# Attention and ternary feed-forward on one core: steps without maxima as one group with a whole product, flags folded to one count, the last split of maxima ahead of VectorE's SBUF work

## The reference

```python
q, k, v = proj(wq, bq), proj(wk, bk), proj(wv, bv)      # (2, 16, 1024, 8) each
attn = softmax(einsum('bhqd,bhkd->bhqk', q, k) / sqrt(16))
a = einsum('bhqk,bhkd->bhqd', attn, v) -> (2, 1024, 128) @ wo.T + bo
x = layernorm(x + a)
h = silu((x @ w1.T) * w1_s) * ((x @ w2.T) * w2_s)        # hidden 512
h = gelu((h @ h1.T) * h1_s);  h = gelu((h @ h2.T) * h2_s)
x = layernorm(x + (h @ w3.T) * w3_s)
```

## Time and profile before

| what | value |
|---|---|
| median of 3 executions | 463.82 us (463.69 to 465.52) |
| the profiled execution, its own time | 464.68 us |
| its span | 462.9 us |
| TensorE busy | 449.7 us, 97% |
| VectorE busy | 399.0 us, 86% |
| ScalarE busy | 361.5 us, 78% |
| GpSimd busy | 87.6 us, 19% |
| granted TensorE clock, mean | 0.992 |

### The profile page before, as it was taken

One profiled execution on the slowest core, in us unless ns is written; L12 is line 12 of the kernel. 1 busy time (PEld: TensorE's weight loads), 2 busy tenths in 40 slices (PEclk: granted clock), 3 DMA queues, 4 the chain that ended last, 5 costly groups with the idle time before them and its releaser, 6 DMA issues.

```text
span 462.9 us, 9462 instructions
## 1 busy us (share of the span) xinstructions
PE 449.7 (97%) x3632; PEld 213.1 (46%) x3632; DVE 399.0 (86%) x450; ACT 361.5 (78%) x670; POOL 87.6 (19%) x138
## 2 busy tenths in 40 slices
PE   8999999999999999999999999999989999999994
PEld 5433333343333333333333333334343478877883
DVE  6899999999999999999999999999944377666736
ACT  3402898989988898998989889999968886677662
POOL 8400000000000000000000001254331081127103
PEclk9999999999999999999999999999989999999998
DMA  6667430500323060051304006031012000000101
GB/s 163 159 189 214 132 117 4 93 4 0 60 37 117 4 92 4 1 75 22 115 12 83 4 1 93 7 44 24 37 22 59 15 14 2 1 1 0 47 1 45
DMA packets 15547, 24.48 MB, mean 53 GB/s; under 512 B 4560, under 2 KB 8400, under 8 KB 15120
## 3 DMA queue, kind: packets, MB, share of 16 engines
q1 hardware_dynamic: 14864, 23.22, 21.8%
q10 hardware_dynamic: 640, 0.66, 0.7%
HBM read 14.82 MB, written 7.47 MB: 48 GB/s over the span
## 4 chain that ended last, share of the span: by engine, by line
PE 81%; DVE 10%; ACT 4%; DMA 1%; issue 1%; POOL 1%; ACTq 0%; POOLq 0%; DVEq 0%
PE ps L1049 32%; PE ps L1103 29%; PE ps L1190 15%; DVE negmax L805 8%; PE ps L1086 2%; ACT arena L547 2%; PE ps L1139 1%; DMA qx<-parts_q 1%; PE ps L1005 1%; ACT v_pad L583 1%; PE ps L1014 1%; PE ps L1073 1%; DMA parts_q<-arena 1%; PE ps L1157 1%; DVE hf L892 0%
## 5 line engine op out<-in xcount | busy, mean ns | idle before, releaser
L805 DVE TENSOR_REDUCE negmax<-ps 128x1 f32<-128x1024 f32 x256 | 309.5, 1223 | 5.6 <-PE ps L1049 2.7
L547 ACT ACTIVATE arena<-ps 128x512 f32<-128x512 f32 x512 | 275.1, 597 | 38.9 <-PE ps L1086 14.4
L1049 PE MATMUL ps<-kx,qx 61*128 61x512 f32 x512 | 186.3, 443 | 1.3 <-DVE negmax L805 0.9
L1086 PE MATMUL ps<-qx,kx 64*128 64x512 f32 x512 | 182.4, 450 | 0.0
L1103 PE MATMUL ps<-arena,v_pad 128*32 128x256 f32 x2048 | 163.7, 392 | 1.1 <-ACT arena L547 1.1
L1049 PEld LDWEIGHTS ps<-kx,qx 61*128 61x128 f32 x512 | 75.3, 184 | 100.4 <-DVE negmax L805 86.4
L1103 PEld LDWEIGHTS ps<-arena,v_pad 128*32 128x32 f32 x2048 | 40.3, 108 | 88.2 <-issue 51.4
L1086 PEld LDWEIGHTS ps<-qx,kx 64*128 64x128 f32 x512 | 75.8, 184 | 8.3 <-issue 5.1
L1190 PE MATMUL ps<-hid,w_high 128*128 128x512 f32 (+1 forms) x296 | 68.2, 387 | 0.8 <-issue 0.4
L1190 PEld LDWEIGHTS ps<-hid,w_high 128*128 128x128 f32 x296 | 54.2, 188 | 12.3 <-issue 0.8
L910 DVE TENSOR_TENSOR hid<-hf,hid 128x512 fp32r<-128x512 f32 x32 | 23.0, 727 | 20.2 <-ACT hid L599 20.2
(11 more groups left out here) (72 smaller groups left out, 228.4 us busy)
## 6 DMA issues: line engine op xcount, KB each, us to landing
kx<-parts_k SPq DMA_DIRECT2D x32, 128.0 KB, 3.7
qx<-parts_q SPq DMA_DIRECT2D x60, 64.0 KB, 3.8
late_sb<-in_late SPq DMA_DIRECT2D x3, 1280.0 KB, 5.7
parts_q<-prt SPq DMA_DIRECT2D x3, 512.0 KB, 4.5
parts_q<-arena SPq DMA_DIRECT2D x3, 512.0 KB, 5.1
xT_sb<-in_xT SPq DMA_DIRECT2D x4, 256.0 KB, 3.5
xT_sb<-arena SPq DMA_DIRECT2D x28, 32.0 KB
prt<-den SPq DMA_DIRECT2D x7, 128.0 KB
```

The costliest lines, as they stand in the source:

```text
L547: nc.scalar.activation(probs[:, n // HG % 2, heads(n), :], ps[:, PLAN["score", n][0], :], ACT.Exp, scale=SCALE).then_inc(exp_done, 1)
L805: nc.vector.tensor_reduce(negmax[:, t // TURNS % 2, h * QT + q:h * QT + q + 1], ps[:, bank:bank + 2, :], AX.XY, ALU.max, negate=True)\
L1049: ins = nc.tensor.matmul(ps[:, MAX_BANK + 2 * (t % 2) + part, :], qx[at, slot, qc, h, q * P:(q + 1) * P], kx[at, slot, h, part * C:(part + ...
L1086: nc.tensor.matmul(ps[:, bank, :], kx[at, slot, h % PAIR, kt * P:(kt + 1) * P], qx[at, slot, qc, h % PAIR, :], start=True, stop=True)\
```

## The change

**Groups.** From half 232 on (`TAIL_HALF`) a group is a whole step: four scores, then the product of the step before with all 512 queries in each of its matmuls. Before that nothing changes. The last turn of maxima moves from half 234 to the first such group, behind its scores.

**Banks.** Two banks that the turns used (4 and 5, `LATE_BANKS`) join the scores' rotation in place of one, and the scores go through five banks in turn. The x1 transposes and the count move to banks 2 and 3.

**Flags.** VectorE flags eight slices, adds them pairwise into one (bf16), flags the other three and adds them too (`fold`). TensorE does one count matmul over the folded slice in place of eleven. The count goes behind step 125 of the 128, the x1 transposes behind steps 121 and 122 (before: 123 and 125).

**VectorE's order.** `norm(0)` waits for the last split of maxima. Both chunks' statistics come first, then both normalisations, then the flags and folds around `split_x1`, then the reduction and `invert(2)`; `norm(2)` goes behind the gate tiles of chunk 1. ScalarE's copies of a unit or of the maxima go between the second and third exponential of a group.

```diff
-FIRST_BANKS, LATE_BANK = [7, 0, 6, 1], 5
+FIRST_BANKS, LATE_BANKS = [7, 0, 6, 1], (4, 5)
...
+TAIL_HALF = 2 * (TAIL - 1)
+GROUPS_ALL = TAIL_HALF + STEPS_ALL - (TAIL - 1)
+TURN_AT = {min(2 * KT * (w - 1) + THALF, TAIL_HALF): w for w in range(1, U_ALL)}
...
+def scores_of(h):
+    if h < TAIL_HALF:
+        return range(2 * h + HG, 2 * h + HG + 2)
+    return range((step_of(h) + 1) * HG, min((step_of(h) + 2) * HG, SCORES))
...
-                order.insert(0, LATE_BANK)
-                last[LATE_BANK] = ("reduced", U_ALL * TURNS)
+                order[:0] = LATE_BANKS
+                last.update({bank: ("reduced", U_ALL * TURNS) for bank in LATE_BANKS})
...
-WO_BANK, X1T_BANK, INEXACT_BANK = [2, 3, 6, 7], [2, 4, 6, 7], 4
+WO_BANK, X1T_BANK, INEXACT_BANK = [2, 3, 6, 7], [2, 3, 6, 7], 2
...
+            def fold(n, done):
+
+                nc.vector.tensor_tensor(nonzero[:, 0:n, :], nonzero[:, 0:n, :], nonzero[:, n:2 * n, :],
+                                        ALU.add).then_inc(flagged, 1)
+                dve.wait_ge(flagged, done)
...
+            dve.wait_ge(max_split, U_ALL)
             norm(0)
             norm(1)
-            flag(0, FLAGGED)
             first_stats(0)
+            first_stats(1)
             invert(1)
             first_apply(0)
+            first_apply(1)
+            flag(0, FLAGGED, 0, 1)
+            fold(4, 2)
+            split_x1(0)
+            split_x1(1)
+            fold(2, 3)
+            fold(1, 4)
+            flag(FLAGGED, SLICES, 1, 5)
+            fold(2, 6)
+            fold(1, 7)
             dve.wait_ge(counted, 1)
-            flag(FLAGGED, SLICES)
-            first_stats(1)
-            dve.wait_ge(counted, 2)
...
-            first_apply(1)
-            split_x1(0)
             invert(2)
-            split_x1(1)
-            norm(2)
...
+            norm(2)
...
-                at = slice(part * HALF, (part + 1) * HALF)
+                at = slice(0 if first else HALF, C if last else HALF)
...
-                for n in range(n0, n1):
-                    ins = nc.tensor.matmul(ps[0:1, INEXACT_BANK, :], ones[:], nonzero[:, n - n0, :],
-                                           start=(n == 0), stop=(n == SLICES - 1))
-                ins.then_inc(counted, 1)
+                pe.wait_ge(flagged, FOLDS)
+                pe.wait_ge(x1_split, 1)
+                nc.tensor.matmul(ps[0:1, INEXACT_BANK, :], ones[:], nonzero[:, 0, :],
+                                 start=True, stop=True).then_inc(counted, 1)
...
             BEHIND = {STEPS - 11: (out_proj, 0), STEPS - 10: (out_proj, 1),
-                      STEPS - 9: (count, 0, FLAGGED), STEPS - 6: (count, FLAGGED, SLICES),
-                      STEPS - 5: (turn_x1, 0), STEPS - 3: (turn_x1, 1)}
+                      STEPS - 7: (turn_x1, 0), STEPS - 6: (turn_x1, 1), STEPS - 3: (count,)}
```

More of the change, by code:

```diff
@@ L78, with step_of, unit_from @@
 HALF = C // 2
-HALVES_ALL = 2 * U_ALL * KT
+STEPS_ALL = U_ALL * KT
 SCORES = U_ALL * KT * HG
 TAIL = (U_ALL * TURNS - TURNS - LEAD + 1) // 2 + 1
-TURN_AT = {2 * KT * (w - 1) + THALF: w for w in range(1, U_ALL)}
+TAIL_HALF = 2 * (TAIL - 1)
+GROUPS_ALL = TAIL_HALF + STEPS_ALL - (TAIL - 1)
+TURN_AT = {min(2 * KT * (w - 1) + THALF, TAIL_HALF): w for w in range(1, U_ALL)}
 def heads(n):
     return ((1, 0, 3, 2), (1, 3, 0, 2))[n // HG >= TAIL][n % HG]
+def step_of(h):
+    return h // 2 if h < TAIL_HALF else h - TAIL_HALF + TAIL - 1
+def scores_of(h):
+    if h < TAIL_HALF:
+        return range(2 * h + HG, 2 * h + HG + 2)
+    return range((step_of(h) + 1) * HG, min((step_of(h) + 2) * HG, SCORES))
+def unit_from(h):
+    return step_of(h) // KT if step_of(h) % KT == 0 and (h >= TAIL_HALF or h % 2 == 0) and h >= 0 else None
 def bank_plan():
@@ L100, in bank_plan @@
     place(("max", 0))
-    for h in range(-2, HALVES_ALL - 2):
-        if h in TURN_AT:
+    for h in range(-2, GROUPS_ALL):
+        if h in TURN_AT and h < TAIL_HALF:
             place(("max", TURN_AT[h]))
-        for n in (2 * h + HG, 2 * h + HG + 1):
+        for n in scores_of(h):
             if n == TAIL * HG:
-                order.insert(0, LATE_BANK)
-                last[LATE_BANK] = ("reduced", U_ALL * TURNS)
+                order[:0] = LATE_BANKS
+                last.update({bank: ("reduced", U_ALL * TURNS) for bank in LATE_BANKS})
             place(("score", n))
[L109 to L118, removed]
+        if h in TURN_AT and h >= TAIL_HALF:
+            place(("max", TURN_AT[h]))
+        w = unit_from(h)
+        if w == 0:
+            plan["pv", w] = held, None
+        elif w is not None:
+            place(("pv", w))
+            order.remove(plan["pv", w][0])
+            order.insert(0, held)
+            last[held] = ("unit", w - 1)
+            held = plan["pv", w][0]
     return plan
 PLAN = bank_plan()
-WO_BANK, X1T_BANK, INEXACT_BANK = [2, 3, 6, 7], [2, 4, 6, 7], 4
+WO_BANK, X1T_BANK, INEXACT_BANK = [2, 3, 6, 7], [2, 3, 6, 7], 2
 GATE_BANKS, GELU_BANK = [(0, 2, 6), (0, 2, 4)], 4
@@ L131 @@
 PIECE = LATE // (ITERS - 1)
-FLAGGED = 8
+FLAGGED, FOLDS = 8, 7
 W_STEPS = range(0, 2 * SLICES, 2)
@@ L555, in copy_max, with copy_unit @@
                 nc.scalar.activation(mT[:, w % 2, :], turned(w), ACT.Copy).then_inc(max_copied, 1)
+            def copy_unit(w):
+                act.wait_ge(pv_done, (w + 1) * KT)
+                nc.scalar.activation(attn_flat[:, w * C:(w + 1) * C], ps[:, PLAN["pv", w][0], :], ACT.Copy)\
+                   .then_inc(unit_out, 1)
             copy_max(0)
-            for h in range(-2, HALVES_ALL):
-                if h in TURN_AT:
+            for h in range(-2, GROUPS_ALL):
+                if h in TURN_AT and h < TAIL_HALF:
                     copy_max(TURN_AT[h])
[L561 to L565, removed]
+                if h < TAIL_HALF and unit_from(h):
+                    copy_unit(unit_from(h) - 1)
+                for n in scores_of(h):
+                    exp(n)
+                    if h >= TAIL_HALF and unit_from(h) and n % HG == 1:
+                        copy_unit(unit_from(h) - 1)
+                    if h >= TAIL_HALF and h in TURN_AT and n % HG == 1:
+                        copy_max(TURN_AT[h])
+                k = step_of(h) - STEPS * (ITERS - 1)
+                if k in W_STEPS and (h >= TAIL_HALF or h % 2 == 1):
+                    n = W_STEPS.index(k)
                     if n == 0:
@@ L568, in _ @@
                     nc.scalar.activation(half(w_high[:, n, :]), w_sb[:, n, :], ACT.Copy).then_inc(w_rounded, 1)
[L569 to L574, removed]
+            warm(ACT.Silu)
+            copy_unit(U_ALL - 1)
             def silu(c, m):
```

41 lines of the change are left out of this document (21 added, 20 removed).

## The result

The changed kernel takes 458.04 us (median of 4 executions, 457.59 to 458.6), the kernel before in the same comparison 464.35 us (463.69 to 465.52). The ratio is 0.9856 with an interval of 0.9835 to 0.9877, so it is faster by 1.2 to 1.7%. Now and then an execution of one and the same kernel takes about 20 us more at a lower granted clock (478 to 479 us at 0.944 to 0.947 in the experiment with four banks), and such executions are left out of the times here. A second comparison later gave 458.68 against 464.99 us, ratio 0.9868 (0.9845 to 0.9891). The profiled execution took 457.77 us with a span of 456.0, the one before 464.68 and 462.9: the span fell by 6.9 us, the median by 6.3.

What follows compares the result with a forecast made beforehand. TensorE and ScalarE hold each other up in the tail. ScalarE: 334.67 + 24.2 work + 1.7 waits = 360.6; last product 361.7, plus 0.2 is 361.9, 5.6 us earlier; median 458.2 us, range 457.0 to 461.0.

Steps and rivals of the forecast that it cites:

- Split ahead of SBUF work: GpSimd's last split of maxima ends at 335.1 us instead of 337.76; TensorE loses pause (1.5 us) and clock fall (1.6).
- One group per step: Last 12 key steps: TensorE changes between scores and products once per step, saving 0.14 us each, 1.7 us.
- Flags: TensorE's eleven count matmuls become one, saving 2.1 us; VectorE's 2048-element addition takes 1.2 us, count margin 0.2 us.
- Norm(2): VectorE's norm(2), moved behind chunk 1's gate tiles, ends 0.5 us before output projection 2 starts; nothing charged.
- Waits: ScalarE's tail waits at two output projections and two x1 turns: 0.33, 0.87, 0.14, 0.37; 1.7 us instead of 7.6.
- 44 exponentials at 0.52 us (22.9): ScalarE's exponentials left in the tail after 334.67 us, the largest part of its 24.2 us of work.
- The 0.2 us that I added for the misfit of the old order: Added to the last product's end, 361.7 to 361.9 us, as replaying the old order ended 0.3 us before the trace.
- The f32 rate for the fold: Rival: VectorE's five additions cost 2.7 us more and the count blocks TensorE; 460.5 us, chance 0.12 to 0.13 as given: 0.13.
- One fall that stays: Rival: TensorE's 1.1 us wait before the last product brings one clock fall, 1.6 us; 459.8 us, chance 0.12.
- A step that stays at 2.25 us: Rival: unseen latency keeps both engines in turn, some eight undisturbed steps lose 1.3 us; 459.5 us, chance 0.12.
- The split no earlier: Rival: GpSimd's last split still ends at 337.76 us, the tail 2.5 us later; 460.7 us, chance 0.05.
- The slow rival: Clock keeps falling on TensorE's longer pause per step, 3.7 us steps, 11 us added; 469 us, chance 0.04.

Runs made afterwards that it cites:

- run 1: Kernel before plus one line: VectorE waits for the last split of maxima before norm(0); 461.81 us, ratio 0.9948.
- run 2: Kernel before plus 24 small unused matmuls on TensorE ahead of the last turn of maxima, filling its pause; 463.3 us, ratio 0.9974.
- run 3: Changed kernel without VectorE's wait for the last split before norm(0); 458.65 us, ratio 0.9881 against the kernel before.
- Run 5: Changed kernel with the last steps in halves again (two scores, half a product), five banks and folds kept; 461.97 us, ratio 0.9942 against the kernel before.
- Run 7: Changed kernel with VectorE's large flag operation done twice ahead of the count; 460.47 us, ratio 0.9906 against the kernel before.
- Run 4: Changed kernel with eleven count matmuls again and no folds, eight behind step 123, three behind 125; 460.15 us, ratio 0.99 against the kernel before.

## Why the prediction was right, and what it mis-sized

The forecast of 458.2 us holds with a median of 458.04, inside the range. The mechanisms that I named are the ones in the trace. The gain in the profile was 6.9 us where I had 5.6, though, and that the median still fits to 0.2 us is luck, as worked out below. Step by step:

- *Split ahead of SBUF work: right.* Four operations of 0.22 us, turn at 335.02 us (forecast 335.25), no fall of the clock, output projection 0 not delayed. Runs 1 to 3 separate its two causes and price the pause and the fall at 1.5 us each (forecast 1.5 and 1.6). Not said was that the flag's new place alone would have removed most of it.
- *One group per step: mechanism right, and larger than I gave it.* A whole product took 1.00 us as set. Run 5 gives 3.23 us, some 2.3 of them for groups, where I had put down 1.7 for changes between scores and products, and carried the 0.17 us waits only inside the walk.
- *Flags: right.* The fold took 1.22 us (forecast 1.2), the second normalisation ended at 346.9 us (347.5), the last fold at 356.4 (357.3), and the margin was 0.3 us (0.2). Run 7 confirms it by its wait of 2.01 us. Run 4 gives 1.80 us for the eleven counts, 2.1 in the forecast.
- *Norm(2): right*, it costs nothing; output projection 2 follows it without a wait.
- *Waits: the sum right, the places not.* I had 0.33, 0.87, 0.14 and 0.37, 1.7 us together; measured were 0.62, 0.69, 0.21 and 0.18, again 1.7. The first output projection cost more than set, since ScalarE was free at 339.32 us and not at 339.67, by the step named next; the scores came as forecast (339.95 against 340.00). The second and the last cost less (0.69 and 0.18 against 0.87 and 0.37). That the sums agree to a tenth is luck.
- *The step that was off: "It then has 44 exponentials at 0.52 us (22.9)".* The 0.52 was a quarter of a merged row of four, 2.08 us. A merged row runs from the first start to the last end, and within a run the instructions overlap. In the changed kernel sixteen run in 7.94 us, the first alone 0.60: (7.94 - 0.60) / 15 = 0.49 us from end to end. (Their starts are 0.48 us apart, and the single durations grow within a run, from 0.59 to at most 0.74 us.) By it a row of four is 0.60 + 3 x 0.49 = 2.07, as seen. So 0.52 is right for a row of four that a wait follows, which is what the kernel before had in each undisturbed step, and why replaying the old order fitted the old trace. Where the waits go, fewer ends stand alone. The changed kernel's 44 exponentials come in five unbroken runs: 44 x 0.49 + 5 x 0.11 = 22.1 us, 0.8 less than set. The three copies between them cost 0.17, 0.51 and 0.49 us from end to end, 0.2 less than set. Together 1.0 us: ScalarE ended at 359.57 us and not at 360.6. The 0.2 us that I added for the misfit of the old order (which was 0.3) wasn't needed either, and 0.1 is rounding. That is the 1.3 us between 28.3 (333.6 to 361.9) and 27.0 us. It is also most of ScalarE's 1.0 us less of busy time.

The Trainium skill, Perfetto Trace Analysis, in its summary of the profiler window per engine type, says that a ScalarE instruction is shown from the ALU through the write's acknowledgement. That fits with durations of 0.60 us and more at a distance of 0.49; read ahead of the prediction, it would have warned me off the quotient.

Why then did the median come within 0.2 us? Two misfits cancel. I had the profiled execution at 459.1 us and it took 457.77, 1.3 less. From that I took off 0.86 us, by which the profiled execution of before lay above its median, but the changed kernel's median lies 0.27 us above its profiled execution: 1.1 more. The median moved 6.3 us where the profiled span moved 6.9. One part of this may be the fall. Over the three comparisons of the experiments, the executions of before with a mean granted clock of 0.991 or 0.992 took 464.25 to 465.83 us (median 464.96), those at 0.994 or 0.995 463.51 to 464.74 (median 464.21). The profiled one was at 0.992 and had the fall. That not each execution has it is likely from this, but the ranges overlap and only profiled ones show where the clock fell, so it isn't shown.

**The rivals.** The f32 rate for the fold is refuted (1.22 us, not 2.3). One fall that stays: refuted, 1.00 throughout with a pause of 0.89 us before the last product. A step that stays at 2.25 us: refuted by 1.99 us, and run 5 shows what would have kept it, the halves. The split no earlier: refuted. The slow rival, a clock that falls again and again, didn't come. The Trainium skill, TensorE: Matmul & The Clock Gate, in A second HAM failure mode, tells of it for a bf16 kernel whose groups cycle PSUM banks; here, with f32 scores, the banks are cycled at each step and the trace disagrees, with 1.00 from 345.60 to 360.62 us.

## What to carry to other kernels

Divide a merged row by its count only where its length stays the same; for a longer unbroken run take off the first whole duration and divide the rest by one less, since the sum over a tail may be off by more than the waits that it is made to find. A small helper operation that the bounding engine waits for (here 0.9 us of GpSimd work) is worth one wait on a neighbour that has time, and the clock's fall behind the pause can cost as much as the pause. Put-in work is free up to the lead that the scores have, and most of what goes beyond shows as a wait of the engine behind it (1.30 us behind the eight counts, up to 0.24 behind half an output projection), so it goes in pieces, and the last piece where the engine waits anyway.

## What the runs showed of the hardware

- **Pause and clock.** Pauses of TensorE of 1.54 us (before) and 2.01 us (run 7) were followed by half clock; those of 0.89 us (changed), 0.86 us (run 5), 0.92 us (run 4) and 0.98 us (run 3) were not, nor was a filled one (run 2). No profile shown here has a pause of TensorE between 0.98 and 1.54 us. Run 7's profiled execution, with a mean granted clock of 0.987, was 1.7 to 2.4 us longer than its other three, at 0.992 to 0.995; where the clock fell in those isn't recorded.
- **GpSimd beside VectorE.** A split operation took 0.22 us alone, 0.68 and 0.54 beside the norms, two-input f32 multiplications (run 3; in the kernel before 0.69 and 0.54), and 2.15 beside the f32-to-bf16 flag, which is nearly as long as the flag itself, 2.30. So of the 2.7 us by which the last split was late before, 0.8 came from the norms and 1.9 from the flag. In run 1 the residual of the weights fell beside the flag instead and took 2.29 us where it takes 1.27; nobody waited for it. The Trainium skill, SBUF — State Buffer, in Who interferes with whom, says that a tensor_scalar in a 2-port mode holds the shared port pair for the whole instruction and a two-input operation with both inputs in SBUF contends with GpSimd's reads: the trace agrees, 2.15 against 0.68.
- **bf16 addition.** 2048 elements with both inputs in SBUF took 1.22 us, 1024 and 512 together 1.14 us: the flags' rate of 0.52 ns per element and 0.16 us fits the first (1.22) and nearly the second (1.12).
- **ScalarE's exponentials.** One of 128x512 from PSUM took 0.60 us alone, each further one of an unbroken run 0.49 us (16 in 7.94 us).
